# When the second experts' weights are loaded, and how many fillers stand before the linear stage

## The reference

```python
h = tok(x)                                   # shifted patches, layer norm, one product
h = h + attn0(layernorm(h))                  # quantised attention, 12 heads
h = h + ffn0(layernorm(h))                   # 4 experts, each token uses one
h = h + attn1(layernorm(h))                  # linear attention ("the linear stage")
h = h + ffn1(layernorm(h))                   # 8 experts, each token uses two

def ffn0(x):   # expert = argmax of a softmax gate
    out = gelu(x @ w1[expert] + b1[expert]) @ w2[expert] + b2[expert]
def attn1(x):  # keys, values and gates of image 0 only; queries of every image
    fw[t+1] = 0.95 * fw[t] + 0.1 * gate[t] * outer(k0[t], v0[t])
    return (q[t] @ fw[t]) @ w_out.T
def ffn1(x):   # the two best of 8 experts, weighted
    out = sum_k p_k * (gelu_tanh(x @ w_fc[e_k]) @ w_proj[e_k])
```

## Time and profile before

| | |
|---|---|
| timed runs | 598.61 us (median of three, 598.5 to 599.84) |
| span of the profiled execution | 604.2 us |
| TensorE matmul busy | 495.1 us (82%) |
| VectorE busy | 319.2 us (53%) |
| ScalarE busy | 206.6 us (34%) |
| GpSimd busy | 154.5 us (26%) |
| DMA | 84.86 MB, mean 140 GB/s |

### The profile page before, as it was taken

The page is one execution under the profiler, slowest core; times in us unless marked ns, Lnnn a source line. Parts: engine busy times, 40 slices in busy tenths (PEclk is TensorE's granted clock), DMA queues, the critical chain, the costliest instruction groups (busy, mean ns, idle before and its releaser), DMA issues.

```text
span 604.2 us, 12487 instructions
## 1 busy us (share of the span) xinstructions
PE 495.1 (82%) x4400; PEld 457.5 (76%) x4401; DVE 319.2 (53%) x1037; ACT 206.6 (34%) x441; POOL 154.5 (26%) x148
## 2 busy tenths in 40 slices
PE   4999999986443596799998399767999999999960
PEld 4999996575442485799997286756999999999950
DVE  1668999788999786122221356892222222222207
ACT  3630014868984164233334052260121112121110
POOL 1592000000001002465433000005444543443220
PEclk9999999999567686999999589879999999999995
DMA  8995000000009123587779900022666655667117
GB/s 314 408 335 160 15 1 1 1 3 1 0 2 312 30 105 118 168 210 192 162 234 322 295 4 0 1 106 59 190 190 192 201 164 164 190 182 211 34 49 291
DMA packets 40659, 84.86 MB, mean 140 GB/s; under 512 B 7270, under 2 KB 23186, under 8 KB 39586
## 3 DMA queue, kind: packets, MB, share of 16 engines
q1 hardware_dynamic: 33218, 72.81, 37.0%
q0 software_dynamic: 7392, 11.41, 8.3%
HBM read 70.33 MB, written 13.86 MB: 139 GB/s over the span
## 4 chain that ended last, share of the span: by engine, by line
PE 69%; DVE 16%; DMA 6%; ACT 4%; issue 2%; another core or an unknown queue 1%; POOL 0%; SPq 0%; DVEq 0%; ACTq 0%; POOLq 0%
PE ps L1137 18%; PE ps L887 14%; PE ps L1113 12%; PE ps L1121 6%; DMA made<-xT,to_i 3%; DVE h L1924 2%; PE ps L827 2%; PE ps L1002 1%; PE ps L974 1%; DVE xT L1771 1%; PE ps L975 1%; PE ps L1104 1%; PE ps L867 1%; PE ps L868 1%; PE ps L852 1%
## 5 line engine op out<-in xcount | busy, mean ns | idle before, releaser
L1137 PE MATMUL ps<-arena,xn 128*128 x696 | 123.1, 327 | 2.1 <-ACT xn L777 2.1
L1137 PEld LDWEIGHTS ps<-arena,xn 128*128 128x128 f32 x696 | 111.8, 190 | 4.2 <-issue 4.0
L515 POOL DMA_INDIRECT xT<-rows,from_i x58 | 56.3, 971 | 175.8 <-DVE from_i L1785 127.5
L530 POOL DMA_INDIRECT made<-xT,to_i x58 | 67.8, 1170 | 100.9 <-DVE xT L1823 65.9
L887 PE MATMUL ps<-arena 128*128 128x192 f32 (+1 forms) x588 | 85.6, 336 | 9.0 <-ACT arena L556 9.0
L887 PEld LDWEIGHTS ps<-arena 128*128 128x128 f32 (+1 forms) x588 | 83.9, 196 | 9.3 <-ACT arena L556 8.6
L1113 PE MATMUL ps<-xn,arena 128*128 128x128 f32 x696 | 87.2, 275 | 3.2 <-DVE xn L1813 3.2
L1113 PEld LDWEIGHTS ps<-xn,arena 128*128 128x128 f32 x696 | 84.9, 192 | 3.5 <-issue 3.5
L780 ACT ACTIVATE xn<-ps 128x384 f32<-128x384 f32 x78 | 32.6, 493 | 144.7 <-PE ps L1123 110.0
L1811 DVE COPY xn<-ps 128x128 f32<-128x128 f32 x58 | 16.9, 292 | 118.9 <-PE ps L1105 98.2
L777 ACT ACTIVATE xn<-ps,b_all 128x128 f32<-128x128 f32 x114 | 30.8, 389 | 63.5 <-PE ps L1123 51.9
(11 more groups left out here) (373 smaller groups left out, 765.6 us busy)
## 6 DMA issues: line engine op xcount, KB each, us to landing
arena<-ffn_a SPq DMA_DIRECT2D x58, 384.0 KB
arena<-ffn_b SPq DMA_DIRECT2D x116, 96.0 KB
arena<-x_blocks SPq DMA_DIRECT2D x16, 384.0 KB, 7.0
arena<-x_strips SPq DMA_DIRECT2D x3, 1536.0 KB, 12.2
arena<-ffn SPq DMA_DIRECT2D x4, 1152.0 KB
rows<-xn SPq DMA_DIRECT2D x8, 384.0 KB, 2.3
arena<-made SPq DMA_DIRECT2D x8, 384.0 KB, 6.6
arena<-tok_w SPq DMA_DIRECT2D x8, 288.0 KB, 7.3
```

The costliest lines, as they stand in the source:

```text
L515: pool.indirect_dma_start(sx[:, k % 6], None, F["src"], bass.IndirectOffsetOnAxis(from_i[:, k:k + 1], 0)).then_inc(sem(f"sx_in{k % 6}"), 16)
L530: pool.indirect_dma_start(F["made"], bass.IndirectOffsetOnAxis(to_i[:, k:k + 1], 0), yo[:, k % 3], None, compute_op=(ALU.add, ALU.bypass)[ ...
L1137: mm = pe.matmul(ps[:, result_bank(k, N), 0:DIM], hT[:, u % 2, 128 * c:128 * c + 128], F["w2"][:, bass.ds(e2 + DIM * c, DIM)], start=(c == ...
```

## The change

In SyncE's list the second experts' weights move behind the read-back of the first experts' rows: first the read-back, then the six first fillings of `w_up`, then the down weights. The weights of the linear stage stay ahead of the read-back. The six fillings are now in the order of the slots, 0 to 5. In TensorE's list 48 fillers become 18.

```diff
             rows_out(F0)
             up_weights(F0)
+            for dst, src in ((wqn, lin_q), (wkT0, lin_kT[0:128]), ...
+                sp.dma_start(dst, src).then_inc(sem("lin_in"), 16)
+            outputs_in(F0)
+            for k in range(6):
+                sp.wait_ge(sem("a_ps0"), 2 * (TILES0 - (TILES0 - 1 - k) % 6))
+                weights_of(F1, k, HID * k)
             for e in range(0, E1, 2):
                 a, b = e * HCH * DIM, (e + 2) * HCH * DIM
                 sp.dma_start(F1["w2"][:, a:b], ffn1_2[:, a:b]).then_inc(sem("ffn_in1"), 16)
-
-            for dst, src in ((wqn, lin_q), (wkT0, lin_kT[0:128]), ...
-                sp.dma_start(dst, src).then_inc(sem("lin_in"), 16)
-            for k in sorted(range(6), key=lambda k: (k - TILES0) % 6):
-                sp.wait_ge(sem("a_ps0"), 2 * (TILES0 - (TILES0 - 1 - k) % 6))
-                weights_of(F1, k, HID * k)
-            outputs_in(F0)
             rows_out(F1)
...
                 turn_rows(2, i, 2)
-            keep_clock(48)
+            keep_clock(18)
             pe.wait_ge(sem("near_xn"), 6)
```

More of the change, by code:

```diff
@@ L450, in _ @@
             up_weights(F0)
+            for dst, src in ((wqn, lin_q), (wkT0, lin_kT[0:128]), (wkT1[0:K1], lin_kT[128:DIM]), (wvT0, lin_vT[0:128]),
+                             (wvT1[0:K1], lin_vT[128:DIM]), (woT, lin_oT), (wgT0, lin_gT[0:128]), (wgT1[0:K1], lin_gT[128:DIM])):
+                sp.dma_start(dst, src).then_inc(sem("lin_in"), 16)
[3 more added lines that the diff above has]
+                weights_of(F1, k, HID * k)
             for e in range(0, E1, 2):
@@ L453, in _ @@
                 sp.dma_start(F1["w2"][:, a:b], ffn1_2[:, a:b]).then_inc(sem("ffn_in1"), 16)
-            for dst, src in ((wqn, lin_q), (wkT0, lin_kT[0:128]), (wkT1[0:K1], lin_kT[128:DIM]), (wvT0, lin_vT[0:128]),
-                             (wvT1[0:K1], lin_vT[128:DIM]), (woT, lin_oT), (wgT0, lin_gT[0:128]), (wgT1[0:K1], lin_gT[128:DIM])):
-                sp.dma_start(dst, src).then_inc(sem("lin_in"), 16)
-            for k in sorted(range(6), key=lambda k: (k - TILES0) % 6):
-                sp.wait_ge(sem("a_ps0"), 2 * (TILES0 - (TILES0 - 1 - k) % 6))
-                weights_of(F1, k, HID * k)
-            outputs_in(F0)
             rows_out(F1)
```

## The result

The changed kernel takes 593.35 us (median of four runs, 588.78 to 594.99), the kernel before takes 599.23 us beside it (median of four, 598.5 to 599.9). The ratio is 0.9893, 95% interval 0.9854 to 0.9932, so the change saves 4.1 to 8.7 us. The span of the profiled execution is 593.2 us, that of before was 604.2.

What follows compares the result with a forecast made beforehand. Between the expert stages small transfers, slowed by weights not yet needed, and then fillers were taken to bound the kernel. 0.61 + 3.77 + 2.6 + 3.0 less 1.9 gave 8.1 us: from 598.6 to 590.5 us, range 588.0 to 593.6.

Steps and rivals of the forecast that it cites:

- buffer wait: After the first experts' last down product: the add behind it, held by a scatter, would start 0.61 us earlier.
- last scatter: First experts' final adding scatter: without weights under way it lands in 3.6 us instead of 7.37, gaining 3.77 us.
- read-back, first piece: Read-back of the first experts' rows: first piece there in 3.64 us instead of 6.56, gaining 2.92 us.
- gaps in VectorE's statistics: VectorE working through the four read-back pieces: later pieces may hold it up, taken as -0.3 us.
- fillers behind `near_xn`: TensorE ahead of L1201: with 18 fillers it waits for `near_xn` instead of fillers, gaining 3.0 us.
- clock of the products: Key and value products: after a 2 to 4 us gap they start at half clock, costing 1.9 us.
- scatter unchanged: Rival: the adding scatter is slow by itself, so 4.4 us of gain go; 594.9 us, chance 0.08.
- The bound for the fourth piece: Last of the read-back's four pieces: arriving each 1.25 us, it may hold VectorE up by 0.5 us or nothing.
- read-back as slow as now: Rival: fillings issued behind the read-back share the DMA engines with it, so 2.6 us go; 593.1 us, chance 0.13.
- forecast: Main case: all gains come and the clock falls at the key and value products, costing 1.9 us; 590.5 us, chance 0.52.
- clock holds: Rival: TensorE keeps full clock into the key and value products, gain 10.0 us; 588.6 us, chance 0.23.
- weights too late: Rival: the moved weights delay `rows_out(F1)` behind them on the queue, making it slower; 605.5 us, chance 0.04.

Runs made afterwards that it cites:

- The repetition: The changed kernel once more, no edit, giving its second trace: 593.77 us, ratio 0.9873, beside 600.98 for the kernel before.
- third trace of before: The kernel before, profiled again without any edit: 595.93 us, one run.

## Why the prediction was right, and where its sizes were off

**The place and the cause.** Right. The transfers between the stages were slow because of weights that nobody needed yet, and moving either half of these away makes the scatter quick. The move alone is at 0.9885 and the fillers alone at 0.9964, so the fillers are not the main cause. Both together are at 0.9893 and 0.9873: that fewer fillers add anything to the move, 3.0 - 1.9 = 1.1 us in the sum, is not shown by the times.

**The sum.** The sum was 8.1 us. By the table, the three segments take 33.04 us in the mean of three traces of before and 25.00 in the mean of two of after: 8.0 us. The timed gains, 5.9 and 7.2 us by the medians, have intervals of 4.1 to 8.7 and about 5.2 to 10.1 us, both with 8.1 inside; where the 1 to 2 us between the segments and the medians go, no run shows. The repetition's median, 593.77, lies just above the range, beside a kernel before that was slower there too (600.98). The terms:

| term | forecast | three traces of before against two of after |
|---|---|---|
| buffer wait | 0.61 | 0.61, 0.97, 0.41 |
| last scatter | 3.77 | 7.91 (mean) - 3.53 = 4.4 |
| read-back, first piece | 2.92 | 5.49 (mean) - 3.3 = 2.2 |
| gaps in VectorE's statistics | -0.3 | -0.6 |
| fillers behind `near_xn` | 3.0 | 3.2, 2.5, 1.5, less 0.05: 2.4 (mean) |
| clock of the products | -1.9 | -1.6 or 0 |

*Buffer wait and scatter* came as forecast, the scatter even to 0.1 us of the 3.6 that I took from the data of a scatter on quiet queues. The scatter's gain came out larger than forecast only because it took longer in the other two traces of before. The rival "scatter unchanged" is out.

*The read-back and the fillers* were sized from a trace of before in which both were at their longest. The first piece took 4.54 to 6.56 us in three traces, and the fillers held L1201 up by 1.5 to 3.2 us: the less, the sooner `turn_rows` gets full clock (in the third trace of before all of it had that). These are the terms that were over-sized: 2.6 and 3.0 were what one execution showed, and a mean over several is 1.6 and 2.4. (The 3.0 also takes the semaphore's 0.1 off twice: VectorE is ready at 354.47, not 354.6.) That the scatter was under-sized by 0.6, and that the clock's 1.9 was 1.6 or nothing, makes up for it, so it is partly luck that 8.1 meets the 8.0 of the segments. The bound for the fourth piece was also a little low: VectorE waited 0.62 and 0.56 us in the two traces of after where I had allowed 0.5 at most. Gaps of over 0.5 us were one of the prediction's signs of being wrong, and the only one that showed; they cost 0.3 us more than the sum had.

*The Trainium skill's rule on rings* (DMA: Bandwidth & Descriptors, Queues, rings and completion order), by which weights behind the read-back on the same queue can't hold it up, agrees with the runs: with the weights held back until after the norm VectorE is done 12.01 us after the first issue, inside the 11.76 to 12.59 us of the traces with weights right behind. The rival "read-back as slow as now" is out.

*The clock* is the step with two answers. Both "forecast" and "clock holds" occurred, in different runs of the same kernel. In seven traces with 18 fillers, TensorE was idle ahead of L1200 (L1201 in some of the kernels) for 2.12, 2.10, 2.11, 1.97 and 1.79 us where the clock fell, and for 1.56 and 0.95 us where it held. Behind L1200 it was idle for 0.98 us in all of them, so from the end of the fillers to the first key product it had only L1200's 0.40 us to do for 3.17 to 3.50 us where the clock fell, and for 2.94 and 2.33 us where it held. With 30 to 48 fillers there was no gap ahead of L1200 and the clock held. Between the two traces of after it is the clock of `turn_rows` that sets the length of the gap: where the clock comes back late, the turned rows and so the 18 fillers end late and the gap is short. By the Trainium skill (TensorE: Matmul & The Clock Gate, Why this matters for your kernels) idle gaps between bursts of matmuls bring half rate back if they last long enough. The order found here, with the five longest stretches losing the clock, fits that; that the length of the stretch alone decides is not shown.

*The moved weights* cost nothing, as forecast; the rival "weights too late" was shown by issuing them 52 us later, not by the change.

**The base and the spread.** Part of what separates one run of after from another lies in stages that the change doesn't touch. The two traces of after are 593.2 and 587.6 us long. Of these 5.6 us, 3.8 are there before the last down product ends (332.03 against 328.25) and 1.6 are the clock of the products. The windows of 236 to 254, at the start of the first experts, of after and then of its second trace:

```profile
236.00:254.00 18.00, 15.16 (x117) 14.04 (x118) 5.89 (x32) 2.29 (x10) 8.95 (x10) 0.76 0.35 92
```

```profile
236.00:254.00 18.00, 15.92 (x135) 14.92 (x134) 5.32 (x26) 4.33 (x17) 10.18 (x11) 0.92 0.51 145
```

The granted clock is 0.76 in one and 0.92 in the other, over 50 us ahead of the first moved instruction. In the traces with 18 fillers where the last down product ended late (330.8 to 332.0) the products lost their clock as well, in those where it ended early (328.3 and 329.8) they didn't. So in these seven traces the two costs come together, and the runs of after spread over 588.8 to 595.5 us. Why an execution falls on the one side or the other is open: no experiment changed it alone.

## What to carry to other kernels

Look at what the DMA engines carry while the chain of waits runs through small transfers: prefetches that are issued early "because they are free" can double the time of a scatter and lengthen a read-back (here 7.9 for 3.5 us and 5.5 for 3.3 us), and putting half of them behind it may be enough. Then ask how late they may be and who really waits for them, the semaphore's first waiter and not the first use of the data. And size the terms from more than one trace of the kernel before, since one execution can have both of its variable waits at their longest; by the traces fillers are best counted so that they end when the awaited engine does, neither before nor after, though the times here don't show that gain.

## What had not been expected of the hardware

- A scatter that adds, issued by GpSimd, landed in 3.44 to 3.56 us in the nine traces where at least half of the weights were out of its way (the same scatter took 7.37 to 8.22 us in the four traces with all weights ahead, DMA share 1.1), so a factor of over two comes from other traffic alone.
- The same kernel's read-back took 4.54, 5.38 and 6.56 us until its first piece with the same transfers issued ahead of it.
- With 18 fillers the following products were slower by 1.6 to 2.8 us in five of seven traces (7.79 or 8.92 us against 6.17), behind an idle gap of only about 2 us, L1200's 0.40 us and another 0.98 us of idling.
